# Encoder stages with their side products in another order, and slot stages whose first bank pair of scores is read by two engines

## The reference

```python
def _encoder_layer(x, iw, ib, ow, ob, l1w, l1b, l2w, l2b, n1w, n1b, n2w, n2b):
    qkv = x @ iw.T + ib                      # 16 heads of 8
    scores = jnp.einsum('bhqd,bhkd->bhqk', q, k) / scale
    attn = jax.nn.softmax(scores, axis=-1)
    o = jnp.einsum('bhqk,bhkd->bhqd', attn, v).transpose(0, 2, 1, 3).reshape(b, s, d)
    o = o @ ow.T + ob
    x = _layernorm(x + o, n1w, n1b)
    ff = jax.nn.relu(x @ l1w.T + l1b) @ l2w.T + l2b
    return _layernorm(x + ff, n2w, n2b)
...
gate_weights = jax.nn.softmax(gate_logits, axis=-1)     # 4 experts, the best 2 per sequence
return jnp.einsum('be,ebsd->bsd', gate_weights * mask, expert_outs)
```

## Time and profile before

| what | value |
|---|---|
| median of 3 runs | 3072.36 us (3067.08 to 3075.82) |
| the profiled execution: its time, its span | 3062.8 us, 3061.1 us |
| PE busy | 2707.2 us (88%) |
| DVE, ACT, POOL busy | 1910.4 us (62%), 1389.4 us (45%), 1094.8 us (36%) |
| granted TensorE clock, mean | 0.951 of full speed |
| costliest lines: L569 (ACT), L604 (DVE) | 415.6 us, 376.8 us |
| matmuls L471, L500, L520 | 241.8 us, 241.0 us, 224.5 us |

### The profile page before, as it was taken

One profiled execution on the slowest core, in us unless ns is written; L12 is line 12 of the kernel. 1 busy time (PEld: TensorE's weight loads), 2 busy tenths in 40 slices (PEclk: granted clock), 3 DMA queues, 4 the chain that ended last, 5 costly groups with the idle time before them and its releaser, 6 DMA issues. The chain is left out here.

```text
span 3061.1 us, 62358 instructions
## 1 busy us (share of the span) xinstructions
PE 2707.2 (88%) x24181; PEld 1791.2 (59%) x24181; DVE 1910.4 (62%) x4325; ACT 1389.4 (45%) x2900; POOL 1094.8 (36%) x1448
## 2 busy tenths in 40 slices
PE   7899699978799977888788899997999989789997
PEld 2344367756467755566455677774666657456664
DVE  7888644556544566743675577765677746566764
ACT  5556144434244434423453355543555534355553
POOL 4788444324344323313112334330222246312222
PEclk9899799999789988988999999998999999999999
DMA  2000200001000001010111000002222201112221
GB/s 82 1 1 1 78 19 19 9 24 31 22 19 20 10 1 36 18 69 26 39 26 34 17 1 1 1 1 72 59 83 75 72 19 30 61 46 75 80 74 47
DMA packets 62498, 107.09 MB, mean 35 GB/s; under 512 B 8138, under 2 KB 47062, under 8 KB 61440
## 3 DMA queue, kind: packets, MB, share of 16 engines
q1 hardware_dynamic: 56832, 94.63, 10.3%
q0 software_dynamic: 5376, 8.47, 1.0%
HBM read 79.66 MB, written 23.86 MB: 34 GB/s over the span
## 5 line engine op out<-in xcount | busy, mean ns | idle before, releaser
L569 ACT ACTIVATE s_sT<-s_R 128x1024 f32<-128x1024 f32 (+2 forms) x448 | 415.6, 947 | 157.7 <-PE s_R L500 157.5
L604 DVE TENSOR_REDUCE s_negm<-s_R 128x4 f32<-128x1024 f32 x320 | 376.8, 1220 | 86.6 <-PE s_R L471 84.4
L471 PE MATMUL s_R<-s_qk 32*128 32x256 f32 (+2 forms) x3584 | 241.8, 382 | 92.2 <-ACT s_sT L569 66.8
L500 PE MATMUL s_R<-s_qA,s_qk 32*128 32x256 f32 (+2 forms) x3584 | 241.0, 382 | 20.9 <-DVE s_negm L604 12.6
L622 DVE TENSOR_TENSOR s_qA<-s_qk,s_OB 128x256 f32<-128x256 f32 x224 | 94.3, 421 | 264.6 <-PE s_OB L543 257.9
L471 PEld LDWEIGHTS s_R<-s_qk 32*128 32x128 f32 x3584 | 159.3, 185 | 142.6 <-issue 122.3
L520 PE MATMUL s_OB<-s_sT,s_v 128*32 128x256 f32 (+2 forms) x3584 | 224.5, 368 | 10.2 <-ACT s_sT L569 6.4
L500 PEld LDWEIGHTS s_R<-s_qA,s_qk 32*128 32x128 f32 x3584 | 163.2, 185 | 106.1 <-issue 102.8
L576 ACT ACTIVATE s_oc<-s_OB 128x256 f32<-128x256 f32 x224 | 85.8, 383 | 268.6 <-PE s_OB L520 264.3
L1519 POOL TENSOR_TENSOR s_pr<-s_pr,s_rinv 128x1024 f32<-128x1024 f32 x64 | 121.1, 1892 | 186.7 <-DVE s_rinv L1630 186.7
L2860 POOL TENSOR_TENSOR all_hT<-s0s_hs,s0s_cb 128x1024 f32<-128x1024 f32 x64 | 150.6, 2353 | 29.2 <-PE s0s_Y L2807 13.8
(11 more groups left out here) (613 smaller groups left out, 6263.0 us busy)
## 6 DMA issues: line engine op xcount, KB each, us to landing
s_wB<-enc_b SPq DMA_DIRECT2D x32, 962.5 KB, 4.8
s_scratch<-s_pk SPq DMA_DIRECT2D x58, 256.0 KB, 2.0
s_qk<-s_scratch SPq DMA_DIRECT2D x232, 64.0 KB
s_wA<-enc_a SPq DMA_DIRECT2D x32, 193.0 KB, 4.2
big<-moe SPq DMA_DIRECT2D x2, 2347.0 KB, 10.8
all_W<-weights SPq DMA_DIRECT2D x2, 2199.5 KB, 13.5
big<-routed SPq DMA_DIRECT2D x2, 2084.0 KB
s_returned<-s_back SPq DMA_DIRECT2D x2, 1024.0 KB
```

What stands on the lines that cost most here:

```text
L471: last = pe.matmul(S[h][:, t * T:t * T + hi - lo], b.qk[rows, r % 2, 0, c, t * P:(t + 1) * P], b.qk[rows, r % 2, 1, c, lo:hi], start=(t == ...
L500: last = pe.matmul(b.R[:, a.turned_at(u, h // 2), :][:, h % 2, a.at(kt)], b.qk[rows, r % 2, 1, c, kt * P:(kt + 1) * P], b.qA[rows, u % 2, ...
L569: act.activation(b.sT[:, u % (a.lag + 1), 2 * p:2 * p + 2, 0:a.width], b.R[:, a.turned_at(u, p), 0:a.width], ACT.Exp).then_inc(s.expd, 1)
L604: ins = dve.tensor_reduce(b.negm[:, u % 2, :, at].rearrange("p t h -> p h t"), S.rearrange("p h (t k) -> p h t k", t=TT), AX_X, ALU.max, n ...
```

## The change

Two edits that don't touch one another.

**1. The encoder's tables and order.** PV stands ahead of the early items, on TensorE and ScalarE; both exponentials stand ahead of the late items on ScalarE; the tables put the short products early and the long ones late (`v`, `y`, `t`, `t1` early; `qk`, `f1`, `f2`, `f3` late). VectorE's addition for f3 goes to the end of the step.

```diff
-    early = {0: [("qk", 1)], 1: [("f1", -2)], 2: [("y", -1)], 3: [("f3", -2)]}
-    late = {0: [("t1", -2)], 1: [("t", -1)], 2: [("f2", -2)], 3: [("v", 1)]}
+    early = {0: [("t1", -2)], 1: [("t", -1)], 2: [("y", -1)], 3: [("v", 1)]}
+    late = {0: [("qk", 1)], 1: [("f1", -2)], 2: [("f2", -2)], 3: [("f3", -2)]}
...
                     if u + 1 < U:
                         slot_scores_pe(pe, g, a, b, u + 1)
+                    if 0 <= u - a.lag < U:
+                        slot_pv_pe(pe, a, b, u - a.lag)
                     for item in a.early(u):
                         other(item)
-                    if 0 <= u - a.lag < U:
-                        slot_pv_pe(pe, a, b, u - a.lag)
...
                     if 0 <= u < U:
                         slot_exp_act(act, a, b, u, 0)
+                        slot_exp_act(act, a, b, u, 1)
                     for item in a.late(u):
                         other(item)
-                    if 0 <= u < U:
-                        slot_exp_act(act, a, b, u, 1)
```

```diff
+def slot_hold_act(act, a, b, u):
+
+    s = b.sems
+    act.wait_ge(s.scored, 2 * u + 1)
+    if u:
+        act.wait_ge(s.maxed, a.maxima * u)
+    act.activation(b.kept[:, 0:a.key_width], b.R[:, a.scores_at(u, 0), :][:, 1, 0:a.key_width], ACT.Copy)\
+       .then_inc(s.held, 1)
...
+def slot_max_dve(dve, a, b, u):
+
+    s = b.sems
+    pairs = [b.R[:, a.scores_at(u, p), :] for p in range(2)]
+    dve.wait_ge(s.scored, 2 * u + 1)
+    if a.maxima == 3:
+        slot_maxima_of(dve, a, b, u, (0,), pairs[0][:, 0:1, :]).then_inc(s.maxed, 1)
     else:
...
+        slot_maxima_of(dve, a, b, u, (0, 1), pairs[0]).then_inc(s.maxed, 1)
+    dve.wait_ge(s.scored, 2 * u + 2)
+    slot_maxima_of(dve, a, b, u, (2, 3), pairs[1]).then_inc(s.maxed, 1)
+    if a.maxima == 3:
+        dve.wait_ge(s.held, u + 1)
+        slot_maxima_of(dve, a, b, u, (1,), b.kept[:].unsqueeze(1)).then_inc(s.maxed, 1)
...
     if u + 1 < a.U:
-        pe.wait_ge(s.maxed, 2 * (u + 1) + 1)
+        pe.wait_ge(s.maxed, a.maxima * (u + 1) + 1)
+        if a.maxima == 3:
+            pe.wait_ge(s.held, u + 2)
...
                 for u in a.steps:
+                    if u + 1 < U:
+                        slot_hold_act(act, a, b, u + 1)
                     for item in a.early(u):
                         other(item)
```

More of the change, by code:

```diff
@@ L188, with __init__ @@
     QUERIES = {None: ((0, 256), (0, 256)), "causal": ((0, 256), (128, 256)), "window": ((0, 192), (128, 256))}
-    def __init__(self, units, early, late, extra, mask=None, first=()):
+    def __init__(self, units, early, late, extra, mask=None, first=(), hold=False):
         self.units, self.U, self.mask = units, units * self.NC, mask
         self.lag = 1 if mask is None else 2
+        self.maxima = 3 if hold else 2
         self.steps = range(-1, self.U + extra)
@@ L197, in __init__ @@
         self.width = sum(self.n)
+        self.key_n = [hi - lo for lo, hi in self.keys]
+        self.key_width = sum(self.key_n)
         self.first = list(first) if first else [("qk", 0), ("v", 0)]
@@ L462, in slot_scores_pe @@
     if u:
[L463 removed]
+        pe.wait_ge(s.maxed, a.maxima * (u - 1) + 2)
     if u >= 2:
@@ L767, in _ @@
                     if u + 1 < U:
-                        for p in range(2):
-                            slot_max_dve(dve, a, b, u + 1, p)
+                        slot_max_dve(dve, a, b, u + 1)
                     for item in a.early(u):
```

57 lines of the change are left out of this document (30 added, 27 removed).

## The result

The changed kernel takes 3020.70 us (median of 4 runs, 3018.32 to 3030.25) against 3073.15 (3067.08 to 3075.82) in the same job: ratio 0.9838, 95% interval 0.9812 to 0.9864. The forecast was 3052, the range 3030 to 3074. The direction was right and the gain is more than twice the 20.3 us of the sum. A second profile of the changed kernel has a span of 3019.9 us.

A forecast was written before the change was run, and what follows sets the result against it. TensorE, busy 88% of the span, was taken as the bound, its waits as what counts. Encoders 21.6 - 2, qk trip -8.3, slot stages +9.0 gave 20.3 us off the median 3072.4: 3052, 8-in-10 range 3030 to 3074.

The forecast's parts named there:

- The diagnosis: Second encoder: TensorE's scores wait for ScalarE's first exponential, 16.7 us in 48 places; long products behind the transposes cover it.
- Full units: Encoder units with all seven pieces, 14 of 16 per encoder: 21.85 instead of 22.62 us, 28 x 0.77 = 21.6 us.
- The start of the turned scores: Encoder steps: not before S + 2.54 (S, the scores' start), held by VectorE's maximum; 0.25 new waiting in c = 0, 1.
- the fourth step: Encoder unit, c = 3: 6.40 us less its 0.17 of waiting gives 6.23.
- The trip of qk: Encoders: later store and loads of qk make the next unit's scores wait; 8.3 us given back, bounds nothing and 28.
- The chain: From S0, a unit's first scores: pk copied at S0 + 6.70, next scores possible at S0 + 15.50, due at S0 + 15.62.
- The late issues of 0.8 to 1.3 us: Both encoders: five loads of qk that start late by that much, costed at 5 x 1.1 = 5.5 us.
- The drains: Stretch from an encoder's last scores to the next stage's first scores or the span's end; the forecast gave it nothing.
- finds bank X free in time: Encoders: VectorE's additions and ScalarE's copies follow TensorE's order; every copy but pk's ends over 1 us before the next product.
- The slot stages: Bank pair freed early by splitting the first maximum: unmasked 5.0, causal 3.2, windowed 0.8, together 9.0 us; bounds -5 and 13.1.
- The late norms of c = 3: Unmasked slot stage, c = 3: VectorE 0.2 to 0.3 late from its norms, so gain 0.24 there against 0.39 in c = 1.
- The first rival: Encoders: the qk trip never counts, landing and copies being short; 8.3 us more come off, 3044; chance 0.20.

The follow-up runs named there:

- enc_hold: The changed kernel with the slot stages' early freeing of the first bank pair (maximum of head 0, copy of head 1) in the encoders too: 3029.56 us, ratio 0.9867.
- encoders only: The changed kernel without the slot stages' hold copy and third maximum, so only the encoders' tables and orders are changed: 3038.07 us, ratio 0.9902 to the kernel before.
- qk_early: The changed kernel with the qk product early and the t1 transposes late again in each encoder unit's first step: 3030.32 us, ratio 0.9871.
- f3_first: The changed kernel with VectorE's residual addition behind f3 put back ahead of the step's layer norms: 3063.07 us, ratio 0.9987.
- c3_only: The kernel before with only v early, f3 late in the encoder unit's fourth step and the addition behind the norms: 3063.13 us, ratio 0.9976.
- spare1: The changed kernel with one small unused load ahead of the four loads of qk, in encoder units from the fourth on: 3031.95 us, a single run.
- spare3: The changed kernel with three small unused loads ahead of the four loads of qk, in encoder units from the fourth on: 3063.87 us, a single run.
- slot_late: The changed kernel with the encoders' order in the slot stages too (PV behind the scores; qk, v, h behind the transposes): 3042.56 us, ratio 0.9908.
- both_hold: The changed kernel with the edits of slot_late and enc_hold together: 3052.37 us, ratio 0.9950.

## Why the prediction was wrong

**The diagnosis held.** The scores waited for the exponential, and with the long product behind the transposes that wait is gone. No product waits for bank X in the steady units.

**Full units: 0.77 a unit forecast, 1.04 measured.** The start of the turned scores was right (S + 2.54; measured 2.56), though for a mixed reason: enc_hold shows 0.1 of gate and 0.16 more of TensorE's own work. What was off lies behind it: I had 2.64 to the next scores, it is 2.53, since the qk product takes 0.96 there (2829.08 to 2830.04) and not the 1.07 that I read from L471's end to L520. In the fourth step it is 6.17, not 6.23. From the fourth unit on 12 whole units in each encoder run at 21.58 where none waits: 0.27 x 24 = 6.5 us.

**The trip of qk: 8.3 forecast, 3.6 and 2.4 measured in the changed kernel's two profiles, 7.8 in "encoders only".** The chain was right to 0.1 us: pk complete at S0 + 6.62 (6.70 forecast; the store starts at once), loads 2.04 later, 6.8 to the scores. But the next unit's scores ask at S0 + 15.41 and not 15.62, and the wait is there in some units only. Summed over the steps in front of the third to the sixteenth unit, the excess over qk_early's same steps is 3.6 us for both encoders, 2.4 in the second execution. The late issues of 0.8 to 1.3 us, 5.5 us of the forecast's 8.3, are missing in these two profiles, for a reason that stays open: the same encoders have five of them in "encoders only", and there the excess is 7.8, near the forecast. The spare loads show that the slack is spent: this term is small by a hair, not by kind.

**The drains: nothing forecast, 10.5 measured.** This is the step that failed most. I wrote that the order of the additions on VectorE follows TensorE's "and finds bank X free in time", and asked of it only whether bank X comes free. Who stands behind a waiting addition I asked for ScalarE's copies and not for this one. The norm of x1 stood behind it. In the drains, where TensorE has nothing else, that was on the path: 5.0 and 5.6 us, of which 4.1 each are this order's and most of the rest lies in stretches where before has the lower clock. In the steady units the same move is what lets the t1 transposes go early at all; without it the encoders' change brings nothing (f3_first: encoders of 360.8 and 359.1 us against 360.7 and 357.7, and longer drains).

**The slot stages: 9.0 forecast, 11.4 measured.** c = 1 gives 0.42 (0.39 forecast), c = 3 gives 0.42 (0.24 forecast), c = 0 and 2 nothing: 6.2 us in the unmasked stage, 3.6 in the causal, 1.6 in the windowed. The late norms of c = 3 cost nothing.

**The sum.** Forecast 19.6 - 8.3 + 0 + 9.0 = 20.3. Measured in the second execution: encoders without the trip 26.4, trip -2.4, drains 10.5, slot stages 11.4, together 45.9; the medians of that job are 44 apart. Of the 25.6 us that the forecast lacks, 10.5 are the drains, 6.8 the encoders' steps, 5.9 the trip and 2.4 the slot stages. The first rival (the trip never counts) comes near for the trip only because no store is late in the changed kernel, and was still short by the steps and the drains.

## What to carry to other kernels

When a product moves to another place, follow on every engine what stands behind the instruction that waits for it, in the drain as well as in the steady loop: here the place of one addition, ahead of or behind a norm, decided 39 of 44 us in the new order of products, while in the old order (c3_only) it and its product's move gave 7. Take a step's length from where products will stand and not from where they stand now; the same product was 0.1 us shorter behind transposes. Before a transfer is put later, measure its slack with small spare issues in front of it; here it was nil, and two stages with shorter units lost 12 and 10 us by the same move. Without slack each late transfer is paid in full: the same encoders paid 2.4 to 3.6 us where none was late and 7.8 where five were.

## What the runs showed of the hardware

Four loads of 64 KB through memory, issued one after the other in 2.84 us, let the waiting scores start 6.5 to 8.0 us after the first issue, median 6.8 (51 waits in spare1 and spare3; 6.76 in the earlier trace rows), 4 us behind the end of the last issue. A store of 256 KB that was issued behind 2.9 MB of weights took 9.9 us instead of 2.0 in the changed kernel, 7.6 to 10.9 in all kernels with that order. Two transposes between PV and the turned scores took 0.38 us where nothing held them; where they show 0.48 (2827.03 to 2827.51), 0.1 is a wait that no row marks: a gate as short as that is seen only when it is taken away. Behind several waits of TensorE of 1.65 to 2.98 us the granted clock was 0.5 for 3.4 us, the level of 1.2 GHz instead of 2.4 (slot_late's causal stage, both_hold's windowed one); behind a wait of 2.56 us in slot_late's windowed stage it stayed at 1.00. So a wait for a load can cost more than its own length: in both_hold 2.9 us in two steps.
